# Attention stage with a searched top-64 threshold on one Trainium2 core: thresholds made tile by tile, finer waits, and small moves in four engines' orders

## What is computed

```python
dots = jnp.einsum('bhid,bhjd->bhij', q, k) * QK_SCALE
dots = jnp.einsum('hg,bgij->bhij', W_pre_th, dots)      # mix the 16 heads
dots = jnp.where(causal[None, None], mask_value, dots)
vk = jax.lax.top_k(dots, TOPK)[0][..., -1:]             # TOPK = 64
dots = jnp.where(dots < vk, mask_value, dots)
attn = jax.nn.softmax(dots, axis=-1)
attn = jnp.einsum('hg,bgij->bhij', W_post_th, attn)     # mix the heads again
out = jnp.einsum('bhij,bhjd->bhid', attn, v)
```

## Time and profile before

| | us |
|---|---|
| median of 3 runs | 4131.17 |
| lowest and highest | 4124.45, 4132.26 |
| the profiled execution | 4126.99 |
| its span, first to last instruction | 4125.2 |
| busy in the span: PE / PEld | 3379.2 / 2149.6 |
| busy in the span: DVE / ACT / POOL | 2947.7 / 2531.9 / 2038.0 |

### The profile page before, as it was taken

The page is one execution under the profiler, slowest core; times in us unless marked ns, Lnnn a source line. Parts: engine busy times, 40 slices in busy tenths (PEclk is TensorE's granted clock), DMA queues, the critical chain, the costliest instruction groups (busy, mean ns, idle before and its releaser), DMA issues. The chain is left out here.

```text
span 4125.2 us, 73074 instructions
## 1 busy us (share of the span) xinstructions
PE 3379.2 (82%) x22948; PEld 2149.6 (52%) x22948; DVE 2947.7 (71%) x6613; ACT 2531.9 (61%) x5828; POOL 2038.0 (49%) x5809
## 2 busy tenths in 40 slices
PE   4999999994678898888888868899888888887766
PEld 3444444441455556655556645555665555665444
DVE  3888777774578888678888867888866888873333
ACT  1334334432478889678888737888976888882111
POOL 0112112223576667577666647766757766671111
PEclk8999999997689999889999968999997999998887
DMA  2122222212455654345555225555434555521000
GB/s 101 67 92 92 82 87 82 82 74 100 121 151 159 174 162 114 85 142 159 167 168 138 72 81 143 168 164 167 120 84 130 166 163 170 136 54 40 20 20 25
DMA packets 362895, 466.35 MB, mean 113 GB/s; under 512 B 30132, under 2 KB 294708, under 8 KB 362168
## 3 DMA queue, kind: packets, MB, share of 16 engines
q1 hardware_dynamic: 362424, 461.02, 38.0%
HBM read 226.57 MB, written 234.36 MB: 112 GB/s over the span
## 5 line engine op out<-in xcount | busy, mean ns | idle before, releaser
L1386 ACT ACTIVATE junk<-D,nt 128x76 int8<-128x76 f32 (+62 forms) x1440 | 1070.6, 746 | 178.6 <-POOL nt L1471 142.1
L1299 PE MATMUL banks<-kr,E 128*128 128x128 f32 (+1 forms) x4672 | 736.9, 308 | 192.8 <-issue 94.6
L1299 PEld LDWEIGHTS banks<-kr,E 128*128 128x128 f32 (+1 forms) x4672 | 630.5, 210 | 302.7 <-issue 279.1
L1272 PE MATMUL banks<-Sg,kpre 128*128 128x109 f32 (+51 forms) x1568 | 649.0, 514 | 18.2 <-DVE D L1598 9.1
L1258 PE MATMUL banks<-kT,qT 64*128 64x343 f32 (+11 forms) x896 | 401.0, 530 | 213.6 <-DVE Sn L1587 161.6
L1409 ACT ACTIVATE AT<-banks 128x512 f32<-128x512 f32 (+3 forms) x768 | 345.3, 478 | 328.2 <-PE banks L1317 164.6
L1677 DVE SCALAR_TENSOR_TENSOR E<-D,vk,E 128x12 f32<-128x12 f32 (+56 forms) x512 | 378.4, 757 | 211.8 <-DVE vk L1633 131.8
L1587 DVE COPY Sn<-banks 128x686 f32<-128x686 f32 (+7 forms) x448 | 376.6, 841 | 142.2 <-PE banks L1259 132.1
L1613 DVE SCALAR_TENSOR_TENSOR W<-SG,sgn,W 128x76 f32<-128x76 int8 (+14 forms) x480 | 412.7, 899 | 84.6 <-POOL W L1487 82.5
L933 DVE RECIPROCAL a_ri<-a_rr 128x512 f32<-128x512 f32 x128 | 429.2, 3353 | 4.4
L1317 PE MATMUL banks<-AT,V 128*64 128x64 f32 x9216 | 367.1, 232 | 61.5 <-issue 46.8
(11 more groups left out here) (188 smaller groups left out, 5600.1 us busy)
## 6 DMA issues: line engine op xcount, KB each, us to landing
score_scratch<-Sn SPq DMA_DIRECT2D x96, 343.0 KB, 3.2
q_scratch<-a_qn SPq DMA_DIRECT2D x32, 512.0 KB, 2.8
v_scratch<-a_vo SPq DMA_DIRECT2D x32, 512.0 KB, 3.6
k_scratch<-a_qn SPq DMA_DIRECT2D x32, 512.0 KB, 2.8
gate_scratch<-a_gs SPq DMA_DIRECT2D x32, 512.0 KB, 2.7
kT<-k_scratch SPq DMA_DIRECT2D x32, 512.0 KB, 4.7
qT<-q_scratch SPq DMA_DIRECT2D x32, 512.0 KB, 6.1
gateT<-gate_scratch SPq DMA_DIRECT2D x32, 512.0 KB, 11.9
```

The lines of the kernel that those rows point to most:

```text
L1272: out = nc.tensor.matmul(bank[:, 0:c], kpre[:].rearrange("p h r -> p (h r)"), Sg[:, g % 3, c0:c1], start=True, stop=not diagonal)
L1299: out = nc.tensor.matmul(ps[5 + i % 2][0:rows, c % 4 * P:(c % 4 + 1) * P], E[:, g % 4, c * P:c * P + rows], kr[:, g % 4, :], start=True, s ...
L1386: nc.scalar.activation(out, D[:, e, 1:1 + n], ACT.Sign, bias=nt[:, r, e:e + 1], scale=-1.0, accum_out=cnt[:, r, e:e + 1]).then_inc(s[f"cnt ...
```

## The change

Four kinds of edit, all in the attention:
1. POOL's `better` makes the next threshold of each tile by one operation with two scalars per partition, 128x1, without the step over `move`; each waits for its own tile's count, and each count on ACT waits for its own tile's threshold.
2. `judge` uses the same form: scale and sign in one operation, add and compare in one, per tile.
3. Two waits for `pick` become earlier ones: count 3 may overwrite `SG` once `sides` has read it (`near`), and `nearest` may overwrite `W` once `closest` has read it (`best`).
4. Orders: PE's `post` of the odd tile always comes behind `slots[0]` (before, in three steps of four, ahead of it); ACT's count 3 comes ahead of `turned`, and the first `exps` between the two counts 1; DVE's `verdict` comes ahead of `slots[2]` and `picked`, `key_mean` goes to the step's start and `residual` to its end; POOL's second `spread` comes behind `first`.

```diff
@@ PE
-                if 0 <= k - 5 < S and not held:
-                    post(2 * (k - 5) + 1)
                 units(G, slots[0])
-                if 0 <= k - 5 < S and held:
+                if 0 <= k - 5 < S:
                     post(2 * (k - 5) + 1)
@@ ACT, count
-                act.wait_ge(s[f"nt{r}"], FP[g // 2] + 1)
+                act.wait_ge(s[f"nt{r}"], FP[g // 2] + 1 if r == 0 else i + 1)
                 if r == 3:
                     if i >= 2:
-                        act.wait_ge(s["pick"], i - 1)
+                        act.wait_ge(s["near"], i - 1)
@@ ACT, the step
-                if 0 <= k - 5 < S and not held:
-                    turned(2 * (k - 5))
                 if searched(k - 2):
                     count(2 * (k - 2), 3)
                     count(2 * (k - 2) + 1, 3)
+                if 0 <= k - 5 < S and not held:
+                    turned(2 * (k - 5))
+                if searched(k - 1):
+                    count(2 * (k - 1), 1)
+                if 0 <= k - 3 < S:
+                    exps(2 * (k - 3))
                 if 0 <= k - 5 < S and held:
                     turned(2 * (k - 5))
                 if searched(k - 1):
-                    count(2 * (k - 1), 1)
                     count(2 * (k - 1) + 1, 1)
                 if 0 <= k - 5 < S:
                     turned(2 * (k - 5) + 1)
                 if 0 <= k - 3 < S:
-                    exps(2 * (k - 3))
                     exps(2 * (k - 3) + 1)
@@ POOL, better
-                pool.wait_ge(s[f"cnt{q - 1}"], 2 * FP[p] + 2)
                 pool.wait_ge(s[f"base{q}"], FP[p] + 1)
-                chain(tt(move[:, q - 1, e], cnt[:, q - 1, e], tab[:, G1 + q - 1, t], ALU.mult))
-                tt(nt[:, q, e], move[:, q - 1, e], base[:, q - 1, e], ALU.add).then_inc(s[f"nt{q}"], 1)
+                for h in (0, 1):
+                    x, y = e.start + h, t.start + h
+                    pool.wait_ge(s[f"cnt{q - 1}"], 2 * FP[p] + h + 1)
+                    ts(nt[:, q, x:x + 1], cnt[:, q - 1, x:x + 1], tab[:, G1 + q - 1, y:y + 1], base[:, q - 1, x:x + 1],
+                       ALU.mult, ALU.add).then_inc(s[f"nt{q}"], 1)
@@ POOL, nearest
-                        pool.wait_ge(s["pick"], i - 1)
+                        pool.wait_ge(s["best"], i - 1)
@@ POOL, judge
+                pool.wait_ge(s["side"], FP[p] + 1)
+                for x in (e.start, e.start + 1):
+                    ts(tie[:, 0, x:x + 1], nt[:, 3, x:x + 1], sgn[:, x:x + 1], SMALL, ALU.mult, ALU.mult)
                 pool.wait_ge(s["pos"], FP[p] + 1)
-                chain(tt(tie[:, 0, e], nt[:, 3, e], sgn[:, e], ALU.mult))
-                chain(ts(tie[:, 1, e], tie[:, 0, e], SMALL, None, ALU.mult))
-                ts(far[:, e], pos[:, e], 15.5, None, ALU.is_gt)
+                chain(ts(far[:, e], pos[:, e], 15.5, None, ALU.is_gt))
                 pool.wait_ge(s["pick"], 2 * FP[p] + 2)
-                chain(tt(tie[:, 2, e], m8[:, e, 0], tie[:, 1, e], ALU.add))
-                chain(ts(tie[:, 3, e], tie[:, 2, e], 0.0, None, ALU.is_equal))
-                tt(bad[:, e], tie[:, 3, e], far[:, e], ALU.add).then_inc(s["bad"], 1)
+                for x in (e.start, e.start + 1):
+                    out = ts(tie[:, 1, x:x + 1], m8[:, x, 0:1], tie[:, 0, x:x + 1], 0.0, ALU.add, ALU.is_equal)
+                chain(out)
+                tt(bad[:, e], tie[:, 1, e], far[:, e], ALU.add).then_inc(s["bad"], 1)
@@ POOL, the step
                     spread(2 * (k - 4))
-                    spread(2 * (k - 4) + 1)
                 if searched(k):
                     first(k)
+                if 0 <= k - 4 < S:
+                    spread(2 * (k - 4) + 1)
@@ DVE, the step
                     closest(k - 2)
+                found = verdict(k - 3) if searched(k - 3) else None
                 scored(G, slots[2])
                 if searched(k - 2):
                     picked(k - 2)
                 if 0 <= k - 3 < S:
-                    threshold(k - 3, verdict(k - 3) if searched(k - 3) else None)
+                    threshold(k - 3, found)
                     select(2 * (k - 3))
```

More of the change, by code:

```diff
@@ L1126, in attention @@
         base = sb("base", [P, 3, 8])
-        move = sb("move", [P, 3, 8])
         off = sb("off", [P, 8])
@@ L1133, in attention @@
         vk = sb("vk", [P, 8])
-        tie = sb("tie", [P, 4, 8])
+        tie = sb("tie", [P, 2, 8])
         far = sb("far", [P, 8])
@@ L1341, in _ @@
                 G = k // 8 + 1
-                held = (k - 5) % 4 == 0
                 slots = [range(0)] * 4
@@ L1362, in _ @@
                     missed(k - 3, ps[2]).then_inc(s["mixed"], 1)
+                if k >= 14 and (k - 14) % 8 == 0 and (k - 14) // 8 < NB:
+                    project((k - 14) // 8)
                 units(G, slots[1])
@@ L1365, in _ @@
                     values((k - 8) // 4, 0)
-                if k >= 14 and (k - 14) % 8 == 0 and (k - 14) // 8 < NB:
-                    project((k - 14) // 8)
                 units(G, slots[2])
@@ L1467, in better @@
                 e, t = cells(p)
-                pool.wait_ge(s[f"cnt{q - 1}"], 2 * FP[p] + 2)
                 pool.wait_ge(s[f"base{q}"], FP[p] + 1)
-                chain(tt(move[:, q - 1, e], cnt[:, q - 1, e], tab[:, G1 + q - 1, t], ALU.mult))
-                tt(nt[:, q, e], move[:, q - 1, e], base[:, q - 1, e], ALU.add).then_inc(s[f"nt{q}"], 1)
+                for h in (0, 1):
[3 more added lines that the diff above has]
+                       ALU.mult, ALU.add).then_inc(s[f"nt{q}"], 1)
                 if q < 3:
-                    pool.wait_ge(s[f"nt{q}"], FP[p] + 1)
+                    pool.wait_ge(s[f"nt{q}"], 2 * FP[p] + 2)
                     tt(base[:, q, e], nt[:, q, e], tab[:, C2 + q - 1, t], ALU.add).then_inc(s[f"base{q + 1}"], 1)
@@ L1535, in _ @@
             for k in range(S + 5):
-                if searched(k - 2):
-                    better(k - 2, 3)
                 if 0 <= k - 3 < S and 2 * (k - 3) % (IB * TPB) < 4:
@@ L1542, in _ @@
                         nc.gpsimd.memset(E[:, g % 4, :], 0.0).then_inc(s["e_zero"], 1)
+                if searched(k - 2):
+                    better(k - 2, 3)
                 if searched(k - 3):
@@ L1709, in _ @@
                     slots = unit_slots(G)[4 * (k % 8):4 * (k % 8) + 4]
+                if k % 8 == 7 and k // 8 + 2 < NB:
+                    key_mean(k // 8 + 2)
                 if k >= 9 and (k - 9) % 4 == 0 and (k - 9) // 4 < 2 * NB:
@@ L1713, in _ @@
                     take(2 * k, k - 3)
-                if k >= 15 and (k - 15) % 8 == 0 and (k - 15) // 8 < NB:
-                    residual((k - 15) // 8)
-                if k % 8 == 7 and k // 8 + 2 < NB:
-                    key_mean(k // 8 + 2)
                 scored(G, slots[0])
@@ L1739, in _ @@
                     inverse(k - 3)
+                if k >= 15 and (k - 15) % 8 == 0 and (k - 15) // 8 < NB:
+                    residual((k - 15) // 8)
 def guess_table():
```

## The result

The changed kernel takes 4154.62 us (median of 4 runs, 4148.08 to 4163.39), the kernel before 4131.22 (4 runs): the ratio is 1.0065 (95% interval 1.0049 to 1.0081). That is 23 us slower by the two medians and 27 by the ratio, where 57 faster was forecast. The time lies outside the range. The profiled execution took 4148.08 us, the lowest of the four, and its span is 4146.2.

A forecast was written before the change was run, and what follows sets the result against it. No engine was taken to bound the attention throughout; the fullest one changes by step. Verdict -25, ACT -20, PE's order -18 + 6, POOL 0 gave -57 us: 4070 us profiled, 4074 us median, range 4010 to 4136 us.

The forecast's parts named there:

- Verdict, -25 us: DVE: flag's load hidden behind the second MAX8, 0.42 us each of 240; shortens 60 steps at k % 8 = 2 and 3.
- Rival 4: DVE: load not hidden behind MAX8, or the branch then stalls longer; the 25 us are gone, 4099 us; chance 0.10.
- POOL, 0 us: POOL's new 128x1 operations at 0.22 us, +0.15 us a step, offset by two waits less in `judge`; zero in sum.
- upper bound of +64 us: POOL's worst case: new operations at `kr`'s 0.372 us, 1.06 us more a step, paid in 60 of 240 steps.
- Rival 2: POOL's new form is dear, +64 us, or PE hides the gains; no change, 4131 us; chance 0.13.
- ACT, -20 us: ACT's counts: three waits shrink by up to 289 us; half of 41 us taken, at k % 8 = 7 and 1.
- (a): ACT: `SG` waits only for `sides`, no longer for the pick; all 68.8 us of that wait go.
- (b): ACT: first tile's threshold is made while the second is counted; most of the 142.1 us wait goes where count rounds adjoin.
- (c): ACT: a count and an `exps` fill the waits for PE's multiplication by V; some 78 of 164.6 us go.
- PE's unit ahead of `post`, -18 + 6: DVE gets units earlier, -18 us at k % 8 = 2 and 3; later `post` and second `turned` lose 6 us.
- Rival 1: ACT's late copy of the odd tile stops PE at the multiplication by V; 4164 or 4154 us; chance 0.11.
- The ceiling: Attention: most that shorter waits can give, 4.5 us a block over 32 blocks, about 144 us, estimated from two blocks.

The follow-up runs named there:

- e3: Kernel before with only DVE's verdict moved, so the flag's load is issued earlier; 4101.04 us, ratio 0.9944.
- e2: Kernel before with only POOL's new forms of `better` and `judge` and the counts' per-tile waits; 4152.19 us, ratio 1.0060.
- e10: Kernel before with the verdict's move and the two finer waits (`near` for `SG`, `best` for `W`); 4103.26 us, ratio 0.9927.
- e1: Changed kernel with POOL's `better`, `judge` and the counts' waits as before; 4133.41 us, ratio 1.0006 against the kernel before.
- e7: e1 with ACT's whole order as before; 4105.14 us, ratio 0.9928 against the kernel before.
- e8: e1 with PE's order as before (`post` of the odd tile ahead of the unit in three steps of four); 4137.38 us, ratio 1.0003.

## Why the prediction was wrong, step by step

- **Verdict, -25 us: right in number and sign, in part by luck.** e3 gives -0.56%, -23 us. The load is hidden, as forecast, but under the `take` and not under MAX8, so the narrow tiles are covered as well. 0.71 us a time went and not 0.42, 170 us and not 101, and a smaller share of it reached the span: 90 us came back as waits for `W` and for the units, which the prediction named as late next. The gain is also not at steps 2 and 3 alone. The two misses in size cancel. Rival 4's delay behind the branch is what it was: DVE's next instruction starts 0.22 us after the branch starts in about 140 cases and 0.53 us in about 100, in the kernel before and in e3 alike.
- **POOL, 0 us: the first step that failed, a term that was sized too small.** The value taken was 0.22 us, near the lower bound, because the operation has one column; the trace has 0.334. In a comparison of 1 and 128 columns (0.334 and 0.372) the columns don't set the time. The upper bound of +64 us was the place to look: by the medians 0.334 is four fifths of the way to it, and the cost is +0.60%, 25 us (e2), half of what that rule makes of it. The medians leave out that operations of this kind are often held up: the sum of `better`'s operations grew by 1.15 us a step in e2, more than the 1.06 of the upper bound. Rival 2 had the price, but as something that only cancels gains.
- **ACT, -20 us: the second step that failed, wrong in sign.** (a) `SG`'s 68.8 us went, and the wait for V is 72.8 us longer (e10 against e3). (b) The wait for thresholds was to fall to under a half. Where each count waits for its own tile and ACT's order is the old one, it is 161.6 us (e2), before 142.1; with ACT's new order it is 277 to 312, because the `exps` that gave POOL time ahead of count 2 was moved away. (c) The wait for V fell by 76 us, as worked out (78), and shortened nothing that the runs show. Against this stands +0.78% for the new order (e1 over e7), which the step left out: it counted what ACT gains by doing counts and an `exps` earlier, and not who waits for `turned`, nor what the `exps` covered where it stood.
- **PE's unit ahead of `post`, -18 + 6: wrong, it is nothing** (e8 and e1 are the same). The row moved as forecast, but less: 185.8 to 155.9 us of DVE's waits for the units, e8 to e1. The other changes put it back, and it is 112.8 before and 123.2 us in the changed kernel, not below 60.
- **Rival 1** named ACT's copy being late for PE, but looked for it at the multiplication by V, with 2.5 us of cover, and for the odd tile's copy. It bites at the next `post`, which needs the bank that holds the even tile. The prediction never asked how many banks `post` has. Its 4154 us is the measured median by chance: it comes from 48 - 25, and the runs have 25 us for the forms and 32 for ACT's order against 30 gained.
- **The ceiling** of 144 us was never near: the best kernels, e7 and e10, gain 30 us. Steps 7 and 3 get shorter in e1, and steps 0 and 4 take more than that back; in the changed kernel 7 and 3 are not shorter either. That steps 0 and 4 would be longer and 2 and 3 not shorter is what the last paragraph of the prediction named as the sign of a wrong forecast.

The parts in the order in which the runs give them: verdict -0.56%, finer waits about -0.17% (not told from none), orders of PE, POOL's `spread` and DVE's others 0 (e7 against e10), ACT's order +0.78%, the forms on top +0.59%: +0.65% in sum. These are the steps of one chain from the kernel before to the changed one, so that they end at the measured ratio says nothing by itself. The check is e2, where the forms alone cost 0.60%.

What is open: how much of `better`'s price is its form and how much its waits per tile, since no kernel had one without the other; how much of POOL's price is PE's clock; and what PE waits for ahead of V.

## What to carry to other kernels

Where a step is moved behind others on its engine, ask who waits for its output and who waits for the buffer that it frees: the second is easy to overlook. Ask too what the moved step covered where it stood. Here the two together cost 0.78%, more than the 0.73% that the rest gave. An operation that fuses two is not cheaper for that; take its duration from the nearest in *form* (how many scalars per partition it reads), not in size, and keep the dear end of the bounds if the engine is near full in some steps. A register load for a branch was cheap to hide: placed ahead of the instructions that end in the branch, it started as soon as its flag was written.

## What the runs showed of the hardware

POOL's small operations have a price by form, and up to 128 columns hardly by size. Medians: 128x2 without scalars per partition 0.195 us, 128x1 with one and an immediate 0.26, with one as an addend and a comparison 0.31, with two 0.334, and 128x128 with one 0.367 in the changed kernel. Their means in a running kernel are higher: 0.438 us for the form with two scalars in the changed kernel, 0.358 for the first 128x2 operation of `better` in the kernel before. The flag's load and the register instruction behind it (0.308 and 0.183 us) stand behind the two MAX8s in DVE's order, and yet in 201 of 240 cases of e3 the load started while DVE was at the `take` ahead of them; DVE is idle under them for 0.9 us in all. And an engine that is busy 66% of a stage was still one to be paid for: 232.5 us of idle additions on POOL cost 40 us of 4127.
